# A graph layer on five engines: the order of the tasks on VectorE, ScalarE, TensorE and GpSimd, with three TensorE tasks cut into parts

## What is computed

```
mask = adj > 0;  x_proj = x @ W1a;  diff = x[:, :, None] - x[:, None, :]
h  = relu(x_proj[:, :, None] + diff @ W1b + b1)        # (graph, node j, node k, 192)
hm = einsum('bjkh,bjk->bjh', h, mask);  deg = mask.sum(-1)
out = layernorm(x + hm @ W2 + deg[..., None] * b2)
```

## Time and profile before

| what | value |
|---|---|
| three runs, median (lowest to highest) | 253.78 us (253.54 to 254.46) |
| profiled execution, first to last instruction (its span) | 253.0 us, the only time the page gives for it |
| busy: PE, DVE, ACT, POOL | 239.2, 230.0, 214.8, 133.1 us |
| PE's weight loads | 190.5 us |
| HBM read and written | 15.63 and 2.10 MB |
| distance from one pair to the next, 42.80 to 183.68 | 14.09 us |

### The profile page before, as it was taken

How to read it: one execution, slowest core, us unless ns; L and a number is a source line. 1 busy time by engine, 2 the same in 40 slices (tenths; PEclk the granted TensorE clock), 3 DMA queues, 4 the chain that set the end, 5 groups by cost and what they waited for, 6 DMA issues and landing times. The chain is left out here.

```text
span 253.0 us, 9425 instructions
## 1 busy us (share of the span) xinstructions
PE 239.2 (95%) x2813; PEld 190.5 (75%) x2813; DVE 230.0 (91%) x810; ACT 214.8 (85%) x636; POOL 133.1 (53%) x288
## 2 busy tenths in 40 slices
PE   7968999999999999999999999999999999999990
PEld 2536687878887978878877878878887879777870
DVE  4797799999999999999999999999999999979853
ACT  2396999898989999898989989898989898988820
POOL 1415252565555574655554564655655555454834
PEclk9997999999999999999999999999999999999997
DMA  6992003501312203031212203031310110000001
GB/s 196 349 352 87 1 3 127 146 4 43 106 45 51 98 22 106 26 106 41 105 41 76 69 20 99 27 105 44 104 45 25 41 29 17 4 21 3 25 21 51
DMA packets 10552, 18.21 MB, mean 72 GB/s; under 512 B 1296, under 2 KB 7696, under 8 KB 10512
## 3 DMA queue, kind: packets, MB, share of 16 engines
q1 hardware_dynamic: 10512, 17.73, 21.7%
HBM read 15.63 MB, written 2.10 MB: 70 GB/s over the span
## 5 line engine op out<-in xcount | busy, mean ns | idle before, releaser
L1287 PE MATMUL ring<-hot,vh 128*128 128x128 bf16 (+9 forms) x768 | 115.8, 254 | 0.9 <-ACT ring L869 0.4
L1287 PE MATMUL ring<-hot,vl 128*128 128x128 bf16 (+9 forms) x768 | 113.9, 251 | 0.0
L1737 DVE SCALAR_TENSOR_TENSOR sums<-ring,sums 128x256 f32<-128x256 f32 (+14 forms) x304 | 104.9, 375 | 8.7 <-PE ring L1287 4.0
L1287 PEld LDWEIGHTS ring<-hot,vh 128*128 128x128 f16 (+1 forms) x768 | 61.0, 102 | 18.9 <-issue 7.9
L874 ACT COPY ring<-u_sb 128x144 f32<-128x144 f32 (+13 forms) x256 | 65.2, 302 | 9.6 <-DVE sums L1737 7.9
L1287 PEld LDWEIGHTS ring<-hot,vl 128*128 128x128 f16 (+1 forms) x768 | 62.2, 103 | 2.8
L631 POOL TENSOR_TENSOR vl<-vf,vh 128x384 f16<-128x384 f32 x32 | 34.4, 1075 | 49.2 <-ACT vf L839 32.3
L869 ACT COPY ring<-u_sb 128x512 f32<-128x512 f32 (+1 forms) x80 | 45.0, 565 | 0.9 <-PE ring L1111 0.4
L1710 DVE TENSOR_SCALAR hot<-slotT 128x944 bf16<-128x944 f16 (+6 forms) x112 | 28.5, 267 | 0.0
L685 POOL TENSOR_TENSOR sums<-taken,sums 128x512 f32<-128x512 f32 x16 | 20.3, 1272 | 11.7 <-ACT taken L891 11.7
L790 ACT CAST maskT<-bx 128x512 bf16<-128x512 f32 x32 | 18.4, 583 | 8.8 <-PE bx L1139 7.7
(11 more groups left out here) (117 smaller groups left out, 470.8 us busy)
## 6 DMA issues: line engine op xcount, KB each, us to landing
adj_sb<-adj SPq DMA_DIRECT2D x16, 512.0 KB, 3.5
x_sb<-x_pairs SPq DMA_DIRECT2D x16, 128.0 KB, 2.3
xT_sb<-xT SPq DMA_DIRECT2D x16, 128.0 KB, 2.4
x_all<-x SPq DMA_DIRECT2D x4, 512.0 KB, 8.1
out<-o_sb SPq DMA_DIRECT2D x16, 128.0 KB, 1.7
wts<-weights SPq DMA_DIRECT2D x1, 417.0 KB, 4.8
cst_general<-general SPq DMA_DIRECT2D x1, 256.0 KB, 2.7
cst_half<-half SPq DMA_DIRECT2D x1, 137.0 KB, 3.2
```

The costliest lines, as they stand in the source:

```text
L1287: return eng.matmul(to if part == "main" else to[g * HT:g * HT + HT], values, selection, start=False, stop=final, skip_group_check=True)
L1737: eng.scalar_tensor_tensor(out=to, in0=view(pair, part, unit, piece), scalar=0.0, in1=to, op0=ALU.max, op1=ALU.add).then_inc(added[part], 1)
```

## The change

Only the order of the tasks differs, and three PE tasks can be issued in parts. The parts of project, unsort_y and gather, with their waits at the first part and their semaphore at the last:

```diff
+            def project(pair, first=0, end=3 * NT):
+
+                if first == 0:
...
+                    eng.wait_ge(permT_copied, pair.n + (1 if pair.last() else 2))
+
+                for step in range(first, end):
+                    t, g = divmod(step, 3)
                     to = bx3[:, t * 2 * O:(t + 1) * 2 * O]
-                    for g in range(2):
+                    if g < 2:
                         eng.matmul(to[:, g * O:g * O + O], sums[pair.side][:, NT + g * NT + t, :], w2ms[scaled(pair)][:, :],
                                    start=(g == 0), stop=False, skip_group_check=True)
...
+            def unsort_y(pair, first=0, end=TILES):
+                if first == 0:
+                    eng.wait_ge(y_copied, pair.n + 1)
+                    eng.wait_ge(permT_copied, pair.n + 1)
...
+            def gather(pair, part, unit, first=0, end=TILES):
+
                 pieces = UNITS[part][unit]
-                eng.wait_ge(hot_ready, NPIECES * pair.n + pieces[-1] + 1)
-                eng.wait_ge(seeded[part], NU[part] * pair.n + unit + 1)
+                if first == 0:
+                    if unit == 0:
+                        eng.wait_ge(vl_ready, 2 * (pair.n + 1))
+                    eng.wait_ge(hot_ready, NPIECES * pair.n + pieces[-1] + 1)
+                    eng.wait_ge(seeded[part], NU[part] * pair.n + unit + 1)
                 side = pair.side
                 wholes, rests = columns(pair, part, unit)

...
                         groups = slice(0, NT) if part == "tail" else slice(g * NT, g * NT + NT)
                         last = put(rests[:, groups, :], g, k, v, every[:, g * NT + k, :, :], k == 0 and v is vh,
                                    k == NT - 1 and v is vl)
-                last.then_inc(gathered[part], 1)
+                if end == TILES:
+                    last.then_inc(gathered[part], 1)
```

PE's body, whose loop now begins at hidden_u:

```diff
             def body(pair, has=always):
                 new, second, third = pair.at(1), pair.at(2), pair.at(3)
-                if has(0):
-                    gather(pair, "main", 6)
-                if has(1):
-                    turn_perm(new)
-                if has(2):
-                    number_slots(second, 0)
-                    number_slots(second, 1)
-                if has(1):
-                    gather(new, "main", 0)
-                if has(2):
-                    sort_x(second)
-                    excess_tail(second)
-                if has(1):
-                    gather(new, "tail", 0)
                 if has(2):
                     hidden_u_main(second)
                     hidden_u_tail(second)
                 if has(1):
                     gather(new, "tail", 1)
-                    gather(new, "main", 1)
-                if has(0):
-                    project(pair)
+                    gather(new, "main", 1, 0, 2)
+                if has(0):
+                    project(pair, 0, 1)
                 if has(1):
-                    gather(new, "main", 2)
+                    gather(new, "main", 1, 2, 3)
+                if has(0):
+                    project(pair, 1, 4)
+                if has(1):
+                    gather(new, "main", 1, 3, 4)
                 if has(2):
                     hidden_v(second)
                 if has(1):
+                    gather(new, "main", 2)
+                if has(0):
+                    project(pair, 4, 6)
+                if has(1):
                     gather(new, "main", 3)
                 if has(0):
-                    unsort_y(pair)
+                    unsort_y(pair, 0, 2)
                 if has(3):
                     keys(third)
+                if has(0):
+                    unsort_y(pair, 2, 4)
                 if has(1):
                     gather(new, "main", 4)
+                    gather(new, "main", 5, 0, 2)
                 if has(2):
                     excess_main(second)
                 if has(1):
-                    gather(new, "main", 5)
+                    gather(new, "main", 5, 2, 3)
                 if has(3):
                     turn_masks(third, 0)
                 if has(1):
+                    gather(new, "main", 5, 3, 4)
                     gather(new, "tail", 2)
                     gather(new, "tail", 3)
                 if has(3):
                     turn_masks(third, 1)
+                if has(1):
+                    gather(new, "main", 6)
+                if has(3):
+                    number_slots(third, 0)
+                if has(2):
+                    gather(second, "main", 0)
+                    turn_perm(second)
+                if has(3):
+                    number_slots(third, 1)
+                    sort_x(third)
+                    excess_tail(third)
+                if has(2):
+                    gather(second, "tail", 0)

```

POOL's body:

```diff
-                older, old, new, second, third = pair.at(-2), pair.at(-1), pair.at(1), pair.at(2), pair.at(3)
+                elder, new = pair.at(-3), pair.at(1)
                 if has(1):
-                    residual(new)
-                if has(2):
-                    corrections(second)
-                if has(-2):
-                    scale(older)
+                    degrees(new)
+                if has(-3):
+                    moments(elder)
+                    centre(elder)
+                if has(0):
+                    low_v(pair, 0)
+                    low_v(pair, 1)
+                    degree_bias(pair)
                 if has(1):
-                    add_taken(new, 0)
-                if has(-1):
-                    moments(old)
-                    centre(old)
-                if has(2):
-                    low_v(second, 0)
-                if has(3):
-                    degrees(third)
-                if has(2):
-                    low_v(second, 1)
-                    degree_bias(second)
+                    corrections(new)
+                if has(0):
+                    residual(pair)
+                if has(-3):
+                    scale(elder)
+                if has(0):
+                    add_taken(pair, 0)

             eng.memset(zeros[:, :], 0.0).then_inc(zeros_set, 1)
             eng.wait_ge(consts_loaded["single"], 16)
             eng.wait_ge(zeros_set, 1)
```

DVE's first tasks:

```diff
+            first_max()
             masks(Pair(0, 0))
             count_masks(Pair(0, 0))
             count_least(Pair(0, 0))
             count_rest(Pair(0, 0))
             sort_key(Pair(0, 0))
+            make_ident()
             ranks(Pair(0, 0))
+            permutation(Pair(0, 0))
+            ranks_above(Pair(0, 0))
             prepare_weights()
-            permutation(Pair(0, 0))
-            first_max()
-            ranks_above(Pair(0, 0))
+            masks(Pair(0, 1))
+            count_given(Pair(0, 0))
             weight_top()
-            count_given(Pair(0, 0))
             first_scales()
+            count_masks(Pair(0, 1))
             select(Pair(0, 0), 0)
             select(Pair(0, 0), 1)
-            masks(Pair(0, 1))
...
```

PE's last tasks:

```diff
@@ -1466,11 +1487,11 @@
             gather(Pair(0, 15), "main", 5)
             gather(Pair(0, 15), "main", 6)
             unsort_y(Pair(0, 14))
-            keep_busy_last(7)
             project(Pair(0, 15))
             add_over()
+            unsort_y(Pair(0, 15))
+            keep_busy_last(7)
             keep_busy_last(2)
-            unsort_y(Pair(0, 15))
```

More of the change, by code:

```diff
@@ L1292, in gather @@
                     steps.sort(key=lambda step: step[0])
+                steps = steps[2 * first:2 * end]
                 slots = [i for i in pieces if whole(i)]
@@ L1842, in body @@
                     add(old, "main", 5)
-                    add(old, "main", 6)
-                    add(old, "tail", 4)
                 if has(1):
@@ L1847, in body @@
                 if has(-1):
+                    add(old, "main", 6)
+                    add(old, "tail", 4)
                     add(old, "tail", 5)
+                if has(1):
+                    count_given(new)
                 if has(0):
@@ L1876, in body @@
                 if has(1):
-                    select(new, 1)
+                    select(new, 3)
+                if has(0):
+                    add(pair, "tail", 2)
+                if has(-2):
+                    statistics(older)
+                if has(2):
+                    sort_key(second)
+                if has(0):
+                    add(pair, "tail", 3)
+                if has(1):
+                    select(new, 4)
+                if has(0):
+                    add(pair, "main", 1)
+            first_max()
             masks(Pair(0, 0))
```

385 lines of the change are left out of this document (184 added, 201 removed).

## The result

The changed kernel takes 257.50 us (median of 20 runs, 253.80 to 260.56), the kernel before 254.92 beside it (20 runs, 253.54 to 256.04). The ratio is 1.0048 with a 95% interval of 1.0025 to 1.0072: slower by half a per cent, some 1.2 us, where 250.7 was forecast. The ratio leaves out runs more than 1.5% above the fastest of their kernel, ten of the changed kernel's twenty (the profiled one, 258.11, among them) and none of the old one's. The profiled execution has a span of 256.3, against 253.0.

What follows compares the result with a forecast made beforehand. The prediction took DVE (VectorE) to set the pace. From 253.78 us it took -3.5 for the loop, +0.5 for the start and -0.1 for the end, giving 250.7 us, with its own range 249.0 to 252.4 at chance 0.45.

Steps and rivals of the forecast that it cites:

- What bounds the kernel: Steady loop: DVE sets the pace, needing 13.64 of 14.09 us a pair, so an order can give back 0.45.
- its stall of 0.21: Steady loop: DVE's waits for gathers, mainly at add main 2 behind the projection, 0.21 us a pair, taken as gone.
- The steady sum, -0.25 a pair: Steady loop: stall -0.21, port -0.08, new ACT stall +0.04, in all -0.25 us a pair, between -0.45 and +0.15.
- The port term: Steady loop: select 0 no longer overlaps GpSimd's add_taken, gaining 0.08 us a pair.
- 14 pairs: -3.5 us: Loop from add main 1 of pair 0 to that of pair 14: -3.5 us, between -6.3 and +2.1.
- I take +0.5: Start: masks 2.46 late because first_max waits for x_sb, mostly absorbed by later DVE waits; +0.5 us, between -0.3 and +2.1.
- The same at 8 would cost within the same ends: Start: a low granted clock at 8, after PE's warm-up matmuls, would cost within -0.3 to +2.1 us.
- End, "-0.1": End: idle-keeping matmuls move behind the last unsort; -0.1 us, between -0.6 and +0.7 (half clock in the projection).
- C: Rival, start: late x_sb carried whole (+2.1), steady part gives nothing; 255.9 us, chance 0.13.
- D: Rival, port: a select issued behind low_v or add_taken, +0.73 in half of 13 pairs, +4.7; 258.5 us, chance 0.09.

Runs made afterwards that it cites:

- f1: Changed kernel with project, unsort_y and the gathers of main 1 and 5 whole in the loop, hidden_v behind main 2, excess_main behind main 5: 262.85 us, 1.0247.
- e1: Changed kernel with only first_max moved back behind ranks_above of pair 0: 255.82 us, 1.0024 of the kernel before.
- h0: c1 with the end put back: last idle-keeping matmuls at their old places, inverse_deviation(14) ahead of the last residual: 253.86 us, 0.9976.
- h1: h0 with first_max back behind ranks_above of pair 0: 253.19 us, 0.9931 of the kernel before.
- h3: The same kernel as d2, run again: 252.68 us, 0.9911 of the kernel before.
- d2: c1 with the start's order put back in first_max, ACT and PE, and keepers and inverse_deviation(14) put back at the end: 251.90 us, 0.9903.
- c1: Changed kernel with ten more idle-keeping matmuls in the start: 254.68 us, 1.0004 of the kernel before.
- c2: Kernel before with sixteen more idle-keeping matmuls in the start and set_banks(0) moved behind the last of them: 252.52 us, 0.9915 of the kernel before.
- h2: The same kernel as c2, run again: 252.66 us, 0.9913 of the kernel before.
- k0: The same kernel as c2, run once more: 252.36 us, 0.9920 of the kernel before.
- c3: Changed kernel with project, unsort_y and the gathers of main 1 and 5 whole, hidden_v ahead of main 2, excess_main ahead of main 5: 271.89 us, 1.0615.

## Why the prediction was wrong, by its own steps

Three terms failed. Against the forecast the profiled span is 6.4 us too long: 2.5 of it is the loop over 14 pairs, 1.8 the start, 1.9 the end.

- **What bounds the kernel**: right. DVE sets the pace, and its stall of 0.21 went. The moved masks are enough for that in f1; that the projection's parts were needed isn't shown.
- **The steady sum, -0.25 a pair**: mis-sized, -0.16. The stall gave 0.20. The port term was to be -0.08; select 0 is back at 0.28, but DVE's busy time grew by 0.05 a pair, part of it in `least` and the count, the rest not found.
- **"14 pairs: -3.5 us"**: mis-sized. Between the adds of pairs 0 and 14 the changed kernel gained 0.98 (195.38 against 196.36). Only the middle is steady. Pairs 0 to 2 lost 0.33, with two waits of 0.5, and pairs 12 to 14, where the list is another, lost 0.28. DVE's waits in the kernel after, from 47 to 61.3 and from 200 to 229 us (us, times, longest):

```profile
DVE steps_ahead L1596 <- PE bx L1122: 0.5, 1, 0.5
DVE sums L1758 <- PE ring L1291: 0.5, 1, 0.5
```
```profile
DVE sums L1758 <- PE ring L1291: 2.7, 3, 1.4
```
  I multiplied a steady figure by pairs that aren't steady.
- **Start, "I take +0.5"**: this step failed in its mechanism, with +2.34 in this execution, above its own upper end of 2.1, and 1.2 to 1.7 at full clock. The masks, forecast at 6.5, came at 5.81. What I credited, that later waits absorb the delay, holds for the late masks alone (0 to 0.7 by e1 and by h0 against h1): ACT's sum, waiting for its load, absorbs them. But I priced only first_max. ACT's sum_chunk(0) ahead of the slots, with PE's number_slots(1) behind sort_x, cost 0.5 to 1.4 at full clock (h1 against h3 and d2, single profiles). "The same at 8 would cost within the same ends" had the clock in one place only: in c1 and f1 it did fall at 8.6 and 10.1, but in after it fell from 18 on, longer than before, for some 0.7 more (33.52 less 30.89 against 31.18 less 29.26), the collisions with add_taken and low_v included.
- **End, "-0.1"**: wrong by 1.9. The swap of inverse_deviation(14) and the last residual, 1.2, I had not seen in the diff; the half clock, bounded at +0.7 in the projection, came in the last unsort_y in this execution: 16.33 against 15.37 in c1, where it did not.
- **The rivals**: C came nearest, 255.9 through the start with a steady part that gives nothing, deciding at 30.5 for add main 1; that add came at 30.0, in the group of three from 29.68. Its number is near by luck: the late x_sb isn't what was carried (e1, h1), and the loop did give 0.6 to 0.9. D's mechanism is real, but met in the start, in single places of 0.7 and 1.2 us, not in half of all pairs.

The ratio's 1.2 us is, as an estimate, -0.6 to -0.9 from the loop, +1.2 from the reciprocal, and some +0.8 left for start and clock together.

The Trainium skill ("SBUF — State Buffer", Who interferes with whom) has a DVE instruction in a two-port mode, or one with two inputs in SBUF, exclude a GpSimd one that reads SBUF, whichever is issued second waiting. The trace agrees: 1.84 against 0.67 for two selects behind add_taken, and in h3 1.36 against 1.27 for an add_taken beside a key that kept its 0.23. It also says ("TensorE: Matmul & The Clock Gate", A second HAM failure mode) that short idle times between groups of matmuls can make the clock swing between its levels; the start agrees, at 0.50 after waits of 0.72 and 1.00, and at 1.00 with these filled.

What stays open: how much of the start's order is ACT's and how much PE's, and why the clock falls at 8, at 18 or at 20 in one execution and not in another. Loads differ too: x_sb, on which DVE's first task waits, ended that wait at 5.48 to 6.90 in the seven profiles with this start.

## What to carry to other kernels

Price a reordering separately for start, loop, drain and end, list by list: what was gained in ten even pairs (1.6 us) was lost in places that run once. Look at the granted clock in the start before moving anything: sixteen matmuls whose results nothing reads bought 2.2 us, more than the loop's whole gain, and the version that beats both kernels is the old order with them, 0.9915, 0.9913 and 0.9920 in three comparisons, level with the repaired new one. When a list is exchanged in two places of a queue, ask of each pair of neighbours that changed sides who waits for the one that is now second; a small reciprocal behind a waiting residual cost 1.2 us at the end.

## What the runs showed that was not expected

- The kernel's time goes with the granted clock from run to run: the changed kernel took 253.80 at a mean clock of 0.995 and 257.37 at 0.973, with one program. With its start kept busy the old kernel's runs lay within 0.5 us (5 runs, c2), 1.1 (6, h2) and 1.1 (6, k0), without that within 2.1, 1.8 and 1.3 on the same chips (17, 17 and 11 runs).
- In the start, idle times of PE of 0.72 and 1.00 went ahead of 7 us at the lower level, and one of 0.41 lies in it; with ten more matmuls there, the level was 1.00 in that stretch in all eight profiles.
- c3 and f1 differ by two places in PE's list, excess_main ahead of main 5 and hidden_v ahead of main 2, and by 9 us: in c3 the bank that excess_main shares with the residual is a wait of 1.16 in each pair.
